# A decoder of two layers on one core: router with its weights stationary, expert biases inside the last expert's products, one pass for the absorbed rest rows, and a different order of steps

## The reference: what is computed

```
# layer 0, attention: 32 heads, low rank (q 192, kv 64), rotary part 64, causal
q = rms_norm(x @ q_a_w) @ q_b_w;  ckv = x @ kv_a_w
kv = rms_norm(ckv[..., :64]) @ kv_b_w
x = layernorm(x + softmax(causal((q_pass k_pass + q_rot k_rot) * scale)) v @ o_w)
# layer 0, cross block: gated adjacency with the 76 largest of 256 similarities a row
x = layernorm(x + (1 - gamma) * x + gamma * symmetric(sigmoid(sim) * (sim >= threshold)))
# layer 0, experts: 7 routed (2 a token) and 1 shared
gate = x @ Wr + br;  probs = softmax over the 2 largest of gate + gate_bias
u = x @ Wup[e] + bup[e];  g = silu(u @ Wgate[e] + bgate[e]) * u
x = layernorm(x + sum_e probs[e] * (g @ Wdown[e] + bdown[e]) + shared)
# layer 1: attention of 16 heads of 16, rotary, causal; a bilinear cross block with the
# context (layernorm and softmax of its similarities); feed-forward 256 -> 1024 -> 256
```

## Time and profile before

| | |
|---|---|
| median of 3 runs | 766.7 us (764.07, 766.7, 768.89) |
| the profiled execution's own time | 768.46 us |
| its span | 766.7 us |
| TensorE busy | 722.3 us, 94% |
| TensorE weight loads | 607.7 us, 79% |
| VectorE busy | 547.7 us, 71% |
| ScalarE busy | 489.4 us, 64% |
| GpSimd busy | 389.1 us, 51% |
| mean granted clock of TensorE | 0.97 |

### The profile page before, as it was taken

How to read it: one execution, slowest core, us unless ns; L and a number is a source line. 1 busy time by engine, 2 the same in 40 slices (tenths; PEclk the granted TensorE clock), 3 DMA queues, 4 the chain that set the end, 5 groups by cost and what they waited for, 6 DMA issues and landing times.

```text
span 766.7 us, 14524 instructions
## 1 busy us (share of the span) xinstructions
PE 722.3 (94%) x4804; PEld 607.7 (79%) x4804; DVE 547.7 (71%) x1737; ACT 489.4 (64%) x1255; POOL 389.1 (51%) x599
## 2 busy tenths in 40 slices
PE   6999999999999999999699999998889999979994
PEld 4677888889888988889588887887778887648884
DVE  2858975898579969998968456558677657756654
ACT  3668764987478855987376556764467767636541
POOL 1458643774188435977646265448622033547630
PEclk9899999999999999999989999999899999989997
DMA  8651004310341002310200210110200001001310
GB/s 282 173 149 41 15 1 124 111 29 1 94 128 41 3 1 56 111 29 1 84 1 1 83 36 25 63 42 15 69 2 3 4 3 43 2 1 33 109 52 27
DMA packets 34082, 40.06 MB, mean 52 GB/s; under 512 B 6540, under 2 KB 26646, under 8 KB 34008
## 3 DMA queue, kind: packets, MB, share of 16 engines
q1 hardware_dynamic: 34008, 39.15, 17.7%
HBM read 29.04 MB, written 1.05 MB: 39 GB/s over the span
## 4 chain that ended last, share of the span: by engine, by line
PE 81%; DVE 7%; POOL 4%; SPq 3%; issue 3%; DMA 2%; ACT 0%; DVEq 0%; POOLq 0%; ACTq 0%
PE bank L1044 72%; PE bank L1058 9%; POOL probs L2144 2%; DVE top_tok L2055 2%; DVE x L1699 1%; SPq L2402 1%; POOL stat L2147 1%; DMA qT<-xT_plain 1%; DVE bn L1733 1%; DMA xT_plain<-in_xT 1%; POOL qT L2147 1%; DVE y L1705 0%; DVE y L1702 0%; DVE g_pair_lo L1702 0%; SPq L2326 0%
## 5 line engine op out<-in xcount | busy, mean ns | idle before, releaser
L2144 POOL TENSOR_SCALAR probs<-probs,soft 128x256 f32<-128x256 f32 (+1 forms) x256 | 104.0, 427 | 47.7 <-DVE soft L1854 46.4
L1497 ACT ACTIVATE probs<-probs,soft 128x256 f32<-128x256 f32 (+1 forms) x256 | 112.9, 444 | 10.4 <-DVE soft L1846 10.1
L1044 PE MATMUL bank<-xT_hi,w_split_hi 128*128 128x512 f32 x256 | 106.2, 415 | 3.9 <-DVE xT_lo L1702 3.4
L2147 POOL TENSOR_TENSOR w_split_lo<-w_raw,w_split_hi 128x512 fp32r<-128x512 f32 (+2 forms) x57 | 72.8, 1288 | 67.8 <-ACT w_split_hi L1420 67.5
L1044 PE MATMUL bank<-xT_lo,w_split_hi 128*128 128x512 f32 x256 | 103.1, 403 | 0.0
L1044 PE MATMUL bank<-keyT,qT 128*128 128x256 f32 (+1 forms) x512 | 90.2, 328 | 1.5 <-POOL qT L2147 1.5
L1846 DVE CUSTOM_DVE_ANT_0 probs<-bank,mask 128x256 f32<-128x256 f32 (+1 forms) x256 | 79.7, 355 | 13.3 <-PE bank L1044 12.4
L1044 PEld LDWEIGHTS bank<-keyT,qT 128*128 128x128 f32 x512 | 80.5, 191 | 10.1 <-POOL qT L2147 2.5
L2147 POOL TENSOR_TENSOR qT<-qT,xT_plain 64x512 f32<-64x512 f32 x44 | 56.3, 1279 | 51.0 <-DMA qT<-xT_plain 37.0
L1420 ACT ACTIVATE qT<-bank 64x512 f32<-64x512 f32 (+1 forms) x96 | 56.7, 590 | 37.5 <-PE bank L1044 36.1
L1044 PE MATMUL bank<-xT_hi,w_split_lo 128*128 128x512 f32 x192 | 77.6, 404 | 0.0
(11 more groups left out here) (225 smaller groups left out, 1864.0 us busy)
## 6 DMA issues: line engine op xcount, KB each, us to landing
qT<-xT_plain SPq DMA_DIRECT2D x88, 64.0 KB, 2.0
w_raw<-in_w_o SPq DMA_DIRECT2D x8, 512.0 KB, 5.6
w_raw<-in_w_nopeT SPq DMA_DIRECT2D x8, 384.0 KB, 3.2
qT<-rope_buf SPq DMA_DIRECT2D x40, 64.0 KB, 2.0
w_raw<-in_w_gateT SPq DMA_DIRECT2D x8, 256.0 KB, 2.7
w_raw<-in_w_upT SPq DMA_DIRECT2D x8, 256.0 KB, 3.4
w_raw<-in_w_downT SPq DMA_DIRECT2D x8, 256.0 KB, 3.8
w_raw<-in_L_ffn_Wup SPq DMA_DIRECT2D x7, 256.0 KB, 2.9
```

Source lines behind the costliest of these rows:

```text
L1044: return t.matmul(out, lhsT, rhs, start=start, stop=stop, skip_group_check=shared)
L1497: ins = s.activation(p[:, at], p[:, at], ACT.Exp, bias=st[:, 0, r:r + 1], scale=-1.0, accum_out=st[:, 1, r:r + 1])
L2144: return g_.tensor_scalar(out, in0, s1, s2, op0, op1)
L2147: return g_.tensor_tensor(out, in0, in1, op)
```

## The change

Four things.

1. w_q: the host repeats the 64 rest rows in w_nopeT (192 to 256 columns a head), so that one call with 128 weight columns gives them on both halves of the partitions. 12 calls a group become 8; the buffer and the load grow.
2. Router: route_lin has the router's weights (8 columns) stationary and streams 512 tokens, 6 matmuls a half; ScalarE copies the 8 x 512 result into a free part of xT (gate_T), and route_gate turns it back with 4 transposes.
3. Biases: route_bias is gone. For the last expert (number 7, the shared one, whose probability is 1) e_down first multiplies the turned probabilities with b_down into the same bank and accumulates its products on it. The first e_down of a half now adds to x instead of y, and waits for route_norm instead of route_bias.
4. Order: NEAR is larger for four engines, and URGENT adds a number to the level of some 120 kinds of steps. The planner's durations of the changed steps are adapted.

```diff
-    NEAR = {"PE": 0.1, "ACT": 0.1, "DVE": 0.1, "POOL": 0.1, "SP": 0.1, "DMA": 0.1, "WAY": 0.0}
+    NEAR = {"PE": 0.1, "ACT": 0.3, "DVE": 0.1, "POOL": 0.3, "SP": 0.5, "DMA": 0.5, "WAY": 0.0}
+    URGENT = {
+        "adj_gate": -29.0, "adj_mask": -10.0, "adj_qk": 27.0, "adj_sim": -7.0, "att_mix": 2.0,
+        "att_stats": -19.0, "consts": 4.0, "ctx1_back": -4.0, "ctx_T": -16.0, "ctx_tok": -4.0, "down": 12.0,
+        "down_rope": 2.0, "e_down": 16.0, "e_gate": 5.0, "e_split": 4.0, "e_u": -1.0, "exp_norm": 2.0,
+        "exp_stats": 23.0, "f_down": 2.0, "ffn_norm": 9.0, "key_swap": -23.0, "late_rows1": -21.0, "norm": 2.0,
+        "out": -16.0, "pT": 1.0, "q": 14.0, "qkT": 4.0, "qk_split": 2.0, "route_T": -8.0, "route_gate": 19.0,
+        "route_norm": -2.0, "route_soft": 7.0, "s": -1.0, "sim_mix": -4.0, "sim_norm": -3.0, "top_split": -1.0,
+        "v1": -2.0, "w_q": -1.0, "zero": 10.0, ("adj_mask", 0): -3.0, ("adj_mask", 3): -2.0,
+        ("adj_sim", 0): -16.0, ("adj_sim", 1): -2.0, ("adj_sim", 2): 4.0, ("adj_sim", 3): -4.0,
...
+        ("out_stats", 0): 8.0, ("pT", 0): 2.0, ("pv", 0): 1.0, ("pv1", 0): 40.0, ("pv1", 2): -19.0,
...
+        ("xT", "attn1"): 6.0, ("xT", "experts"): -4.0,
+    }
...
             level[step] = (sum(us + self.HOP for _, us, _ in self.parts[step]) + self.ahead[step]
+                           + self.URGENT.get(step[0], 0.0) + self.URGENT.get(step[:2], 0.0)
                            + max((level[o] for o in after[step]), default=0.0))
...
-        stage(("w_q", g), "PE 2.4, ACT 1.3, DVE 1.3, POOL 0.8", ("load", g), *before,
+        stage(("w_q", g), "PE 1.7, ACT 1.3, DVE 1.3, POOL 0.8", ("load", g), *before,
               holds=[bank("absorb", g, left=(("w_q", g), "DVE"))])
...
-        stage(("route_gate", h), "PE 1.6, DVE 2.5", *[("xT", "experts", b) for b in halves(h)], ("split", "router", 0),
+        stage(("route_lin", h), "PE 1.45, ACT 0.6", *[("xT", "experts", b) for b in halves(h)], ("split", "router", 0),
+              holds=[bank("route_lin", h, left=(("route_lin", h), "ACT"))])
+        stage(("route_gate", h), "PE 0.5, DVE 2.7", ("route_lin", h),
               holds=[bank("route_gate", h, left=(("route_gate", h), "DVE"))])
         stage(("route_soft", h), "DVE 0.9, ACT:exp 0.3", ("route_gate", h))
         stage(("route_norm", h), "DVE 0.5", ("route_soft", h))
         stage(("route_T", h), "PE 0.4, DVE 0.5", ("route_norm", h), holds=[bank("route_T", h, left=(("route_T", h), "DVE"))])
-        stage(("route_bias", h), "PE 2.1, DVE 1.3", ("route_T", h),
-              holds=[bank("route_bias", h, i, left=(("route_bias", h), "DVE")) for i in range(TH // TB)], items=2)
 
...
-            stage(("e_down", e, h), "PE 2.85, DVE 1.9", ("e_split", e, h), ("split", U_EXPERT + e, 2),
-                  ("route_bias", h),
+            stage(("e_down", e, h), "PE 4.85, DVE 1.9" if e == E_ROUTED else "PE 2.85, DVE 1.9", ("e_split", e, h),
+                  ("split", U_EXPERT + e, 2), ("route_T" if e == E_ROUTED else "route_norm", h),
                   holds=[bank("e_down", e, h, i, left=(("e_down", e, h), "DVE")) for i in range(TH // 2)],
                   ahead=8.4 * expert_halves_ahead(e, h), items=2)
...
-    RAW, SPLIT = GH * (QLR + 2 * KVLR + D) + 2 * GH * DR, 3 * DC * D
+    RAW, SPLIT = GH * (2 * P + 2 * KVLR + D) + 2 * GH * DR, 3 * DC * D
...
-    probs_eT = [xT[0:NE, i, 0:HALF] for i in range(NHALF)]
+    probs_eT, gate_T = ([xT[0:NE, i, j * HALF:(j + 1) * HALF] for i in range(NHALF)] for j in range(2))
...
                 for i in range(GH):
-                    mm(out[:, 0, i, :], nope[:, i, 0:P], k_lat[:, i, :])
-                    for at in (0, QREST):
-                        ins = mm(out[at:at + QREST, 1, i, :], nope[:, i, P:], k_lat[:, i, :], shared=True)
+                    for c in range(2):
+                        ins = mm(out[:, c, i, :], nope[:, i, c * P:(c + 1) * P], k_lat[:, i, :])
                 ins.then_inc(absorbed.sem, 1)
             elif name == "w_v":
...
-            elif name == "route_gate":
+            elif name == "route_lin":
                 h, = k
                 w.wait_ge(*split_lo["router", 0])
                 w.wait_ge(*latest(xT_lo, [("experts", b) for b in halves(h)]))
-                out = wait_bank(("route_gate", h))[:, 0:TH * NE].rearrange("p (t e) -> p t e", e=NE)
-                for i, tile in enumerate(tiles_of[h]):
-                    ins = mm3_chunks(out[:, i, :],
-                                     [(xT_pair[:, c, tile * P:(tile + 1) * P], w_router[:, c, :]) for c in range(DC)])
+                out = wait_bank(step)[0:NE, :]
+                mm3_chunks(out, [(w_router[:, c, :], xT_pair[:, c, h * HALF:(h + 1) * HALF])
+                                 for c in range(DC)]).then_inc(route_ready.sem, 1)
+            elif name == "route_gate":
+                h, = k
+                w.wait_ge(*route_copied[h,])
+                out = wait_bank(step)[:, 0:TH * NE].rearrange("p (t e) -> p t e", e=NE)
+                for i in range(TH):
+                    ins = transpose(out[:, i, :], gate_T[h][:, i * P:(i + 1) * P])
                 ins.then_inc(route_ready.sem, 1)
             elif name == "route_T":
                 h, = k
...
-            elif name == "route_bias":
-                h, = k
-                w.wait_ge(*route_T_copied[h,])
-                w.wait_ge(*landed("router"))
-                for i in range(TH):
-                    if i % TB == 0:
-                        out = wait_bank(("route_bias", h, i // TB))
-                    ins = mm(out[:, i % TB * D:(i % TB + 1) * D], probs_eT[h][:, i * P:(i + 1) * P], b_down[:, :])
-                    if i % TB == TB - 1:
-                        ins.then_inc(bias_ready.sem, 1)
...
                 w.wait_ge(*e_g_lo[e, h, DC - 1])
+                if e == E_ROUTED:
+                    w.wait_ge(*route_T_copied[h,])
+                    w.wait_ge(*landed("router"))
                 for i in range(TH // 2):
                     out = wait_bank(("e_down", e, h, i))
                     for j in range(2):
-                        at = slice((2 * i + j) * P, (2 * i + j + 1) * P)
-                        ins = mm3_chunks(out[:, j * D:(j + 1) * D], [(gp[:, c, at], we[:, 2, c, :]) for c in range(DC)])
+                        at, part = slice((2 * i + j) * P, (2 * i + j + 1) * P), out[:, j * D:(j + 1) * D]
+                        if e == E_ROUTED:
+
+                            mm(part, probs_eT[h][:, at], b_down[:, :], True, False)
+                        ins = mm3_chunks(part, [(gp[:, c, at], we[:, 2, c, :]) for c in range(DC)], e != E_ROUTED)
                     ins.then_inc(e_down_ready.sem, 1)
             elif name == "qkv":
                 b, i = k
...
+            elif name == "route_lin":
+                h, = k
+                w.wait_ge(*route_ready[step])
+                copy(gate_T[h][:, :], bank_of(step)[0:NE, :]).then_inc(route_copied.sem, 1)
...
-            elif name == "route_bias":
-                h, = k
-                for i, b in enumerate(halves(h)):
-                    w.wait_ge(*bias_ready[h, i])
-                    tt(batch_rows(y, b), two(bank_of((*step, i))), batch_rows(x, b), ALU.add).then_inc(route_done.sem, 1)
...
-                w.wait_ge(*latest(route_done, [(h, i) for i in range(TH // TB)]))
                 for i in range(TH):
                     t = h * TH + i
                     w.wait_ge(*e_down_ready[e, h, i // 2])
                     if h in summed_by:
                         w.wait_ge(*e_added[summed_by[h], h, i])
                     stt(y[:, t, :], bank_of(("e_down", e, h, i // 2))[:, i % 2 * D:(i % 2 + 1) * D], probs_e[:, t, e:e + 1],
-                        y[:, t, :], ALU.mult, ALU.add).then_inc(e_added.sem, 1)
+                        (y if h in summed_by else x)[:, t, :], ALU.mult, ALU.add).then_inc(e_added.sem, 1)
                 summed_by[h] = e
             elif name == "exp_stats":
...
-        "w_nopeT": q_b[:, :, :DN].transpose(2, 1, 0),
+        "w_nopeT": np.concatenate([q_b, q_b[P:]])[:, :, :DN].transpose(2, 1, 0),
```

More of the change, by code:

```diff
@@ L700, in write_program @@
     xT_ready = signal("xT_ready", keys("xT"))
-    route_ready = signal("route_ready", [s for s in ORDER["PE"] if s[0] in ("route_gate", "route_T")])
-    bias_ready = signal("bias_ready", keys("route_bias", range(TH // TB)))
+    route_ready = signal("route_ready", [s for s in ORDER["PE"] if s[0] in ("route_lin", "route_gate", "route_T")])
     e_u_ready = signal("e_u_ready", keys("e_u", range(DC)))
@@ L738, in write_program @@
     xT_hi = signal("xT_hi", keys("xT"))
+    route_copied = signal("route_copied", keys("route_lin"))
     route_exp = signal("route_exp", keys("route_soft"))
@@ L787, in write_program @@
     route_T_copied = signal("route_T_copied", keys("route_T"))
-    route_done = signal("route_done", keys("route_bias", range(TH // TB)))
     e_u_lo = signal("e_u_lo", keys("e_u", range(DC)))
@@ L953, in bank_left @@
```

(10 more changed lines are left out.)

19 lines of the change are left out of this document (18 added, 1 removed).

## The result

Before 766.7 us (median of 5 runs, 764.07 to 769.24), after 762.76 us (761.68 to 763.51): ratio 0.9933, 95% interval 0.9912 to 0.9954. That is 3.9 us less where 15.9 were forecast. The time lies in the range of 736 to 766, near its end, and the change is smaller than the 1% that was to be told from none. The profiled run of after took 763.51 us with a span of 761.7.

The account below looks back on a forecast made before the run. TensorE was taken as the bound in full stages, with waits on VectorE in four layer passages. Edits 8.5 us (3.7 + 1.7 + 3.1) plus order 7.4 made 15.9 off 766.7, so 751 us, range 736 to 766.

Parts of the forecast that it names:

- w_q: Absorbed rest rows: 24 instructions a group become 16, saving 0.62 us in each of groups 2 to 7, 3.7 us.
- At the start: Groups 0 and 1, ahead of transposes waiting for ScalarE's rows: nothing counted, 1.3 us gain as the far end.
- The load of 512 KB: w_nopeT's load per group grows from 384 KB in as many issues: hidden, as DMA engines are busy 15 or 16%.
- Router: Each half of the router falls from 2.68 to 1.82 us on TensorE, 1.7 us saved; 0.3 lost if the copy is awaited.
- The clock behind the router: 512-column streaming keeps full clock behind both router halves: 3.1 us saved, ends 0 and 3.1.
- all three slow stretches: Low clock in 384 to 388, 400.4 to 404 and 420.7 to 424.5 us, costing 1.4, 1.7 and 1.7 us.
- The third: Slow stretch from 420.7 to 424.5 us, behind the second half's biases: 1.7 us, expected to go away with the biases.
- Biases: Eight instructions a half move into expert 7's products: 0 net, ends -1.7 and +1.9 us.
- The searched order: New NEAR and URGENT: 7.4 us gained, 6.4 from idle time in passages and 1 for one slow stretch avoided.
- four passages: Layer-to-layer stretches where TensorE waits, 19.1 of its 27.1 us idle; a third, 6.4 us, was taken as gain.
- Rival B: The searched order gives nothing: 758.2 us, up to 766 if the clock falls and the copy is awaited; chance 0.22.
- C: Rival: the searched order gives nearly all of the passages' idle time, 740 us or less; chance 0.10.
- D: Rival: a top-k on VectorE lands in the passage into the experts, 774 to 776 us, slower; chance 0.10.

Follow-up runs that it names:

- e1: The kernel before with only the new w_q form, planner duration and order unchanged: 5.2 +/- 1.9 us less than before.
- e3: The changed kernel in its own order with the old w_q form: ratio to before 0.9950, 1.3 +/- 2.3 us above the changed kernel.
- e7: The changed kernel in its searched order with old w_q and old router products, biases in their new place: 3.5 +/- 1.0 us less than before.
- e4: The changed kernel in its own order with the old router products: ratio to before 0.9922, 0.8 +/- 2.4 us below the changed kernel.
- e11: The w_q and router edits in the order of before, route_bias kept as its own step: 2.1 +/- 2.0 us below e5.
- e5: All three edits (w_q, router, biases) in the order of before, changed only where it has to be: ratio to before 0.9943.
- e6: Router edit and moved biases in the order of before, w_q in the old form: 2.5 +/- 1.7 us slower than before.
- f15: e5 with matmuls without use filling the same six waits as f14: 2.7 +/- 2.1 us below f14.
- f14: e11 with matmuls without use added ahead of six waits: 1.4 +/- 2.0 us above e11.
- f13: The changed kernel with old w_q for groups 0 and 1 and matmuls without use ahead of five waits: 757.4 us, ratio 0.9870.
- e2: The changed kernel with empty URGENT and old NEAR, so all edits without the search: 772.7 us, 4.4 slower than before.
- e10: The changed kernel with 16 useless matmuls ahead of xT(experts, 2)'s wait and 5 ahead of route_lin(1)'s: 2.5 +/- 2.2 us below the changed kernel.
- e12: e5 with 8 useless 512-column matmuls ahead of e_down(7, 1)'s wait for g_pair_lo: 4.5 +/- 2.0 us below e5.

## Why the prediction was wrong, step by step

**w_q: right.** 3.7 us in six groups, measured 4.0 in e1's trace and 5.2 +/- 1.9 in time. At the start, where I counted nothing with a far end of 1.3, the clock was lower with the shorter groups in the new order (0.61 to 0.74 against 0.87 to 1.00); whether that cost anything is open. The load of 512 KB landed in 3.7 us. In the new order the edit shows only 1.3 +/- 2.3 (e3) or 2.5 +/- 2.0 (e7 against e4).

**Router: its durations right, its worth not.** 1.39 us for the six and 0.34 for the four transposes (380.47 to 380.81) against 1.38 and 0.44. But I took the saving as paid in full. In e11 TensorE reaches u_pair_lo and probs_e sooner and waits 1.9 and 0.6 us for them (1.9 for each in e5 and e6, with the biases moved too), where before has no such wait. Both halves stand next to stretches where VectorE is busy nearly all the time: 3.48 of 4 and 3.39 of 3.6 us in the earlier trace rows. I had written that an instruction pays nothing ahead of a wait for another engine, and then did not apply it here. In the new order half 1's normalised rows came later with the new router, as shown above. With the clock: forecast 4.8, measured 1.3 +/- 2.5 in the old order and -0.8 +/- 2.4 in the new one.

**The clock behind the router: right as a clock, not as time.** Behind route_lin(0) the clock stays at 1.00, as assumed, and in e11 it is 1.00 all the way from 374 to 425 us: all three slow stretches of the earlier trace rows are gone. The third is gone there with the biases still in their old step, so it can't be put down to the biases, as I did. I asked only what the router does to the clock, and not what TensorE did before it. Behind the waits the six themselves ran at the low clock: 2.53 us for route_lin(1) in after and 2.51 for route_lin(0) in e11, where the 24 small ones took 2.68.

**Biases: the step that failed in size.** Forecast 0, with ends of -1.7 and +1.9. One by one between products they take 0.62 us a tile instead of 0.48 and put 0.11 on the next product and 0.09 on the one ahead: 6.0 us a half instead of the 2.85 of another expert's (446.57 to 449.42 us in after), so 3.15 for what cost 1.92. In the old order e_down(7, 1) took 10.6 us where it had taken 4.5 (e5 against e11, 4.4 us more from the first route_lin to the first qkv). Of these 6.1 us I had allowed for 1.92 and, at the low clock, 1.9 more; the rest is the wider spacing of single pairs, and that the step now stays at the low clock to its end. The searched order avoids this: e_down(7, 1) comes behind qkv. With the waits filled (f15 against f14) the move costs nothing, it gains 2.7 +/- 2.1, and no run shows from what.

**The searched order: the term that carried the error.** Forecast 7.4. Given the same edits, new against old order is 0.8 +/- 2.0 us (after against e5), and 2.1 +/- 2.0 with waits filled in both (f13 against f15). On the old forms with the biases moved it is 3.5 +/- 1.0 (e7). Two assumptions failed. I took before's order for the one that the planner would make again with the new durations; e2 shows that it would be 772.7 us, so most of the search's 9.6 us went into getting back to where before's order was. And I measured the room by the idle time in four passages. There the forecast of 6.4 came true, 6.9 us less, but the idle time did not go, it moved: 5.8 us (4.37 and 1.41) opened between 386 and 394, with a low clock behind it that e10 prices at 2.5. I had also held that no order can shrink VectorE's work in a passage. Part of its busy time there is no work: four instructions that take 1.4 us elsewhere are 6.9 of the 16.7 us counted from 522 to 539 in before:

```profile
529.92 6.89 DVE L1699 TENSOR_SCALAR x<-y,bn,stat 128x256 f32<-128x256 f32 x4
```

**Sum.** With measured terms: w_q -5.2, router -1.3, biases' move in the old order +2.1, order -0.8, together -5.2; measured -5.1 +/- 1.6 by the ratio. It closes because the terms are steps of one chain (before, e1, e11, e5, after). Each has an error of about 2 us, so signs of router and order are not settled. Against the forecast the order is short by 6.6 us, router and clock by 3.5, the biases by 2.1; w_q gave 1.5 more. Rival B (the order gives nothing, up to 766 if the clock falls and the copy is waited for) comes nearest; I had given it 0.22. Its second half did not happen: behind route_lin(0) the clock stayed up, and TensorE does not wait for the copy. That 762.8 lies inside the range says little for the working: the range reached to 766 only for that second half. C and D did not happen: the last MAX8 is at 268 us, 329 in before.

## What to carry to other kernels

Take the saving of an instruction at its spacing only where the engine has no wait behind it; in a passage paced by another engine, follow the gain to the next wait, and take nothing until you have found where it is paid. When durations are handed to a greedy planner, changed durations alone can make a bad order out of a good one (8.8 us here): run the edit in the frozen old order first, since it prices edit and order apart. Idle time that goes from one passage can open in the next; add it up over the whole kernel. Where a slow clock stands in a trace, ask whose pace the stretch goes at before filling the idle time ahead of it: two such fillings gave 2.5 and 4.5 us, and those in the passages of the old order nothing that shows. Where VectorE sets the pace, compare its instructions with the same ones elsewhere in the trace before you take its busy time for work.

## What was not expected of the hardware

With instructions of 8 rows in between TensorE stayed at the low clock for all of a 10.6 us step although it issued without a gap (e5), and the very same sequence ran at full clock for 6.0 us where TensorE had been busy ahead of it (after, e12). In e6, behind 2.17 us of idle time, it began at full clock and fell. A 256-column product of 8 rows took 0.24 us in a row of eight and 0.31 alone between others, with 0.11 more on the next. One and the same wait of 2.17 us was followed by the low clock in before and by the full one in e1. And four VectorE instructions of 128x256 took 1.4 us in one place and 5.4 to 9.0 in another, with GpSimd at work beside them.
